# Reordering the first three batch elements at the start of a fused attention and mixture-of-experts kernel

## The reference

```python
# x, ctx: (8, 256, 256); D = 256, 16 heads of 16, FF = 1024, 8 experts, top 2
# block 0 (pre-norm)
h = layernorm(x);  x = x + attention(h, h, causal=True)
h = layernorm(x);  x = x + attention(h, ctx, causal=False)
h = layernorm(x);  x = x + relu(h @ w1 + b1) @ w2 + b2
# block 1 (post-norm)
x = layernorm(x + attention(x, x, causal=True))
x = layernorm(x + attention(x, ctx, causal=False))
x = layernorm(x + moe(x))          # softmax router, top 2 of 8 experts, gelu
# attention: Q, K, V projections with bias, softmax(Q K^T / 4) V per head, output projection with bias
```

## Time and profile before

| | |
|---|---|
| median of 3 runs | 1194.17 us (1192.85 to 1195.81) |
| profiled execution | 1193.72 us, of which span 1192.0 us |
| PE busy | 1067.3 us, 90% of the span |
| DVE busy | 850.7 us, 71% |
| ACT busy | 767.9 us, 64% |
| POOL busy | 521.1 us, 44% |
| mean granted PE clock | 0.969 of full |

### The profile page before, as it was taken

One profiled execution on the slowest core, in us unless ns is written; L12 is line 12 of the kernel. 1 busy time (PEld: TensorE's weight loads), 2 busy tenths in 40 slices (PEclk: granted clock), 3 DMA queues, 4 the chain that ended last, 5 costly groups with the idle time before them and its releaser, 6 DMA issues. The chain is left out here.

```text
span 1192.0 us, 28185 instructions
## 1 busy us (share of the span) xinstructions
PE 1067.3 (90%) x9419; PEld 899.8 (75%) x9419; DVE 850.7 (71%) x2558; ACT 767.9 (64%) x1607; POOL 521.1 (44%) x736
## 2 busy tenths in 40 slices
PE   7788888889999999999989989988989999999950
PEld 6466656668888888886767667766789999999950
DVE  2777888877766666667767677674548887888846
ACT  4365576667766666656556665655458988988932
POOL 4355556423222213445667246542423545354544
PEclk9799999999999999999999999999989999999985
DMA  8656756755355444355756856651647777787764
GB/s 165 97 83 156 87 99 97 97 73 77 51 64 90 55 59 55 64 98 97 110 75 103 131 108 99 101 89 42 255 143 230 239 231 241 225 252 230 242 163 145
DMA packets 112047, 152.43 MB, mean 128 GB/s; under 512 B 23233, under 2 KB 95425, under 8 KB 105537
## 3 DMA queue, kind: packets, MB, share of 16 engines
q1 hardware_dynamic: 101712, 138.64, 55.0%
q0 software_dynamic: 8352, 10.80, 4.7%
q10 hardware_dynamic: 1872, 1.60, 1.1%
HBM read 78.39 MB, written 21.62 MB: 84 GB/s over the span
## 5 line engine op out<-in xcount | busy, mean ns | idle before, releaser
L1091 ACT ACTIVATE probs<-s 128x384 f32<-128x384 f32 (+1 forms) x512 | 264.6, 540 | 140.8 <-PE s L839 130.6
L1173 DVE TENSOR_REDUCE neg_max<-s 128x2 f32<-128x512 f32 x256 | 168.8, 689 | 66.6 <-PE s L811 59.7
L839 PE MATMUL s<-q_stack,k_stack 98*128 98x256 bf16 (+1 forms) x1024 | 175.8, 261 | 20.1 <-ACT probs L1091 18.6
L670 POOL TENSOR_SCALAR_AFFINE_SELECT probs<-probs 128x256 f32<-128x256 f32 x256 | 105.8, 422 | 166.1 <-ACT probs L1091 165.5
L1170 DVE CUSTOM_DVE_ANT_0 s<-s,mask_qk 128x256 f32<-128x256 f32 x256 | 114.6, 447 | 54.6 <-PE s L808 44.3
L839 PEld LDWEIGHTS s<-q_stack,k_stack 98*128 98x128 bf16 x1024 | 88.6, 99 | 47.8 <-ACT probs L1091 31.7
L861 PE MATMUL pv<-probs,v 128*32 128x256 f32 (+1 forms) x2048 | 110.1, 355 | 1.7 <-POOL probs L670 1.4
L1583 PE MATMUL moe<-rows_hi,e_w_hi 128*128 128x256 f32 x368 | 103.2, 281 | 2.2 <-DVE rows_lo L1700 2.2
L1583 PE MATMUL moe<-e_w_hi,e_hidden_hi 128*128 128x256 f32 x368 | 104.6, 284 | 0.0
L1704 DVE TENSOR_TENSOR e_hidden_lo<-e_hidden,e_hidden_hi 128x512 fp32r<-128x512 f32 x92 | 77.5, 842 | 37.0 <-ACT e_hidden_hi L1665 36.0
L1583 PE MATMUL moe<-e_w_lo,e_hidden_hi 128*128 128x256 f32 x368 | 102.8, 279 | 0.0
(11 more groups left out here) (241 smaller groups left out, 3013.2 us busy)
## 6 DMA issues: line engine op xcount, KB each, us to landing
w<-in_expert_w SPq DMA_DIRECT2D x26, 1024.0 KB, 5.2
k_stack<-k_part SPq DMA_DIRECT2D x192, 128.0 KB, 4.3
q_stack<-q_part SPq DMA_DIRECT2D x180, 128.0 KB, 5.9
w_next<-in_expert_w SPq DMA_DIRECT2D x22, 1024.0 KB, 5.3
rows<-slots_x SPq DMA_DIRECT2D x25, 256.0 KB, 2.7
slots_x<-filler SPq DMA_DIRECT2D x8, 518.0 KB, 4.5
cT<-in_context SPq DMA_DIRECT2D x16, 256.0 KB, 6.3
e_b<-in_expert_b SPq DMA_DIRECT2D x24, 128.0 KB
```

The costliest lines, as they stand in the source:

```text
L670: pool.affine_select(out=blocks, in_=blocks, compare_op=ALU.is_ge, fill=0.0, base=0, pattern=[[0, TILES], [1, P]], channel_multiplier=-1). ...
L839: last = pe.matmul(dst[:, kt * S:kt * S + S - q0], k[:, kt * P:(kt + 1) * P], q[:, q0:S], start=True, stop=True)
L1091: act.activation(probs_of(n, hd)[:, 0:width], s2[hd % 2][:, 0:width], ACT.Exp, scale=SCALE).then_inc(probs_ready, 1)
L1173: dve.tensor_reduce(neg_max[:, :, hd], src[:].rearrange("p (t s) -> p t s", t=TILES), AX_X, ALU.max, negate=True).then_inc(s1_free, 1)
```

## The change

```diff
-WARM = 40
+WARM, WARM_NEXT = 31, 8
...
-SECOND = {"ln": -3.0, "T": 1.0, "q": 8.0, "k": 7.0, "v": 9.0}
+SECOND = {"ln": -3.0, "T": 1.6, "q": 8.0, "k": 7.0, "v": 9.0}
+THIRD = {"ln": 13.0, "T": 18.0, "q": 25.0, "k": 24.0, "v": 29.0}
...
+    if n == 2:
+        steps = [(THIRD["ln" if kind == "apply" else kind] - 2 * SLOT if kind in THIRD or kind == "apply" else at, kind, lane, arg) for at, kind, lane, arg in steps]
...
-    steps = [(1.5, "fetch", 0, "rows")]
+    steps = [(4.0, "fetch", 0, "rows")]
...
                 if lane == 1 and c == 0:
-                    idle(WARM)
+                    idle(WARM_NEXT)
...
-                if c == 0 and lane < len(k_stack) - 1:
-                    ones_rows(lane + 1)
+                if c == 0 and 1 <= lane < len(k_stack):
+                    ones_rows(lane)
```

## The result

The changed kernel takes 1205.29 us (median of 11 runs, 1199.92 to 1211.66), the kernel before 1194.44 us beside it (11 runs, 1190.88 to 1197.09). The ratio is 1.0095, 95% interval 1.0075 to 1.0115, or +11.3 us. The prediction said 1198.0, at most 1201.5. The profiled execution after took 1205.29 us, its span 1203.5.

A forecast was written before the change was run, and what follows sets the result against it. Bound: the DMA stream up to the first Q stack's landing, then DVE up to the second shift (SP's small DMAs with call 1's maxima). -0.9 + 2.2 + 3.0 = +4.3 on 1193.7 gives 1198.0 us; range 1191.5 to 1201.5.

The forecast's parts named there:

- the landing: First Q stack arriving, which frees part 0 of q1 on ACT: from 29.59 to 30.9, by -0.9 and +2.2 us.
- the second stretch: DVE from 30.40 to the shift of call 1: idle time 10.3 us against 7.3, so +3.0 us.
- The nine fewer idle transposes: Start on PE: 0.113 us each, 1.0 us in all, of which 0.9 us earlier on the DMA stream.
- The row fetch: Moved behind x3 into a full DMA stream, ahead of the last Q stack DMAs: 2.2 us later landing, 0 if Q goes ahead.
- Rival 2: Both DMA queues share from 15.3, the Q stack lands near 28.8: +2.2 us, 1195.9 in all; chance 0.18.
- `k1` half a us later: On ACT, from q0 before T1: the delay costs nothing, since part 0 of q1 waits for the landing.
- First shift near 52.8: SP's small DMAs carrying the maxima of call 0 come near 52.8, against 45.31 before.
- 18 us between the shifts: From the shift of call 0 to that of call 1, near 70.7: 18 us instead of 21.3.
- they take 2 us longer: Upper bound for the second slot: PE at clock 0.50 for all sixteen maxima and its heads, making +3.0 into +5.
- rival 4: Stacks of call 2 become the limit, landing near 71.5, and PE at half clock adds 2: +7.1, 1200.8; chance 0.12.
- Every us by which the shift of call 1 moves arrives at the end: Third slot, 20.82 us, is unedited, so the second shift's delay is the whole loss and nothing is added behind it.
- Eight idle transposes instead of forty: On PE behind v1: the first maximum could start 1.7 us earlier, but DVE isn't ready; 0.3 us, then replaced by ln2.

The follow-up runs named there:

- the experiments with the fetch and with Q first: Kernel before with only the row fetch behind the fetch of x3: 1.0024; kernel before with only part 0 of q0 ahead of T1 on ACT: 1.0021.
- the mended kernels: Kernel before with q0 before T1, 31 and 27 idle transposes, ones behind V of call 1: 1.0005; also x3 fetched later: 1.0006; or with THIRD: 1.0030.
- the experiment with the ones: Kernel before with only the rows of ones of stacks 1 and 2 made behind V of calls 1 and 2: 1198.88 us, 1.0031.

## Why the prediction was wrong

The direction was right and so were most of the places, the sizes were not: 4.3 us were forecast and 11.3 came. Three steps failed: the landing (+1.3 forecast, +2.8 measured), the second stretch (+3.0 forecast, +4.4 measured, mostly for PE's low clock and the ones), and the step that put the loss behind the second shift at nothing (4 to 6 us).

1. *Landing at 30.9: came at 32.4.* Two of its terms were mis-sized. The nine fewer idle transposes (-0.9) gave 0.27 in after's execution (the K stack was issued at 12.77 for 13.04) and 0.94 in the one with the fetch moved back. The forecast priced a transpose at 0.113 us, the pace of the later forty; the 31 of after took 6.49 us, 0.21 each. Over all profiles 31 took 4.98 to 6.49 us (mean 5.9) and 40 took 6.32 to 7.10 (mean 6.7), so 0.8 is right on average and after's profile was at the poor end. The row fetch, "2.2 us if it is served in order of issue", is what it cost alone; in after it cost 3.0, where the last Q piece moved beside it in turns and the fetch itself moved more slowly, with a gap at its start. Rival 2 (the queues share, landing near 28.8) had the turns, but only one Q piece of six took part in them, and it had the landing early where it came late.
2. *`k1` half a us later, "which is hidden"*, missed that Q pieces among the K pieces delay the K stack: `k1` came 1.6 us later. With the ones and the forty idle transposes behind `k1` and `v1` this costs 2.5 us; in after these runs show nothing that it costs.
3. *First shift near 52.8: came at 53.96.* The distance from part 0 of `q1` is 21.56 us against 21.9 forecast. This stretch, with 1.7 us for POOL (1.56) and 2.9 for `k2` (2.64), was right.
4. *18 us between the shifts: 19.90.* The ones were mis-sized (1.4 us forecast, 2.5 measured), and no term stood for ACT's copy of the second shift: 3.58 us of waiting against 2.04, behind an exponential that waits for PE's product of the probabilities with V (2.79 us against 1.51). `v2` did run at full clock (1.89 us at 53.36 on PE's timeline), but the maxima and heads behind it did not (clock 0.54 in 58 to 73); the forecast kept that case only as an upper bound, "they take 2 us longer". The part from the landing to the second shift grew by 4.4 us where 3.0 were forecast. That the stacks of call 2 set the end here (rival 4) isn't seen: no wait of PE between the landing and the second shift is put down to a DMA.
5. *"Every us by which the shift of call 1 moves arrives at the end"*, and no more: right for the order of work, wrong for the time. The third slot is 20.80 us, but later 4.3 us more are lost in one profile and 1.9 in the other, both against before's first, and 4 to 6 on average. In the first profile (+11.6 us against +4.3 forecast) the miss is 1.2 us by the first shift, 2.0 more by the second and 4.3 behind it, less 0.2 by which the forecast's sum was above its own second shift at 70.7.
6. *Eight idle transposes instead of forty, "worth 0.3 us"*: right up to the second shift (it is 0.08 us apart with 8 and 40), but for the whole 40 of them again in after gave back some 3 us, and 31 and 8 in before cost 0.24%, of which the nine fewer at the start aren't the cause (31 and 40: 1.0007). Both are at the edge of what the intervals allow.

What stays open is why 4 to 6 us are lost behind the second shift, where the order of work is untouched. The mean of the clock's measure is 8.4 us higher after than before, and 5.1 us of that lie in the start (6.83 + 6.83 against 5.12 + 3.42 from the windows of low clock). Among the 110 executions of before whose clock is on record, one us more of this measure goes with 0.67 us more of time (correlation 0.79); by that, an estimate, 8.4 us go with 5.6 of the 11.3. No experiment sets the clock by itself, so this is argued and not shown. A delay alone doesn't raise the measure (56 idle transposes: 36.3). Fewer idle transposes, moved ones, `THIRD` and the late fetch each raise it (38.4, 40.0, 38.3 and 38.1, against 36.0 to 36.6 for before beside them). Only for some of them does the time outrun the shift: 31 and 8 idle transposes (shift -1.3, time +2.9 by the ratio) and the late fetch (+1.2 and +2.9), but not the ones alone (+4.8 and +3.7) or `THIRD` alone (+2.8 and +1.6).

## What to carry to other kernels

A transfer that is free ahead of an empty stretch isn't free in a full one. To price it there, write down the order in which all queues issue: here the pieces moved mostly in that order, so all that is issued ahead of the piece somebody waits for counts, whichever queue it is on, and a large fetch issued just ahead of the last piece counts whole or a little more. Compare executions from the same starting point: two profiles of nearly the same kernel began their stacks 0.4 to 0.7 us apart. Setup work on an engine (here the rows of ones) should stand in a gap that the profile shows on that very engine; one position later it held back the first exponential, and one earlier a part that everything waited for. Work that fills idle time, such as the idle transposes, becomes a wait of its own when what stands in front of it comes late. And idle transposes whose removal moves no wait can still pay through the granted clock elsewhere, so such an edit needs the timed ratio and not only the trace of the stretch.

## What the runs showed of the hardware

- Stack pieces of 128 KB with 1 KB packets, issued on two queues, moved one after the other in their common order of issue at 0.12 to 0.14 MB per us (all stack pieces of call 0 in before, after, and the experiments with the fetch and with Q first, but for one pair issued 0.07 us apart). For call 1 the mended kernels broke that order: a Q piece issued at 29.04 moved ahead of a K piece issued at 28.12. In before, ACT's queue was asked at 30.46 and moved nothing until 34.6, when what SP had issued earlier was through.
- A fetch with 7 KB packets on one queue and a piece with 1 KB packets issued 0.39 us behind it on the other moved equal numbers of packets (42 and 40, 32 and 33). The fetch moved 0.42 MB per us alone and 0.23 to 0.30 so.
- The wait on a stack's landing ended 1.5 to 1.7 us behind its last packet: in before the second queue's data ran out at 27.94 and the wait ended at 29.59, in after at 30.87 and 32.40.
- The same 31 idle transposes at the start took 4.98 to 6.49 us in eleven profiled executions.
- The clock falls or doesn't fall at two places of the program, 101 to 103 and 195 to 201 us behind the second shift, from execution to execution of one kernel: both in the second profile of before, neither in the first.
- The 32 matmuls of the probabilities with V took 1.51 us at full clock (before) and 2.79 at 1.2 GHz (after), the 8 of `q1` 1.89 at full clock (before) and 3.12 with the clock down for most of them (the experiment with the ones).
